# A mixed attention and expert kernel: W2 of all experts kept in SBUF, one pipeline round fewer in the GELU stage, and the SiLU stage's scores brought by transfers instead of matmuls

## What is computed

```python
t = t + landmark_attention(ln(t))       # 16 landmarks, 6 Newton steps for an inverse
t = t + ffn_gelu(ln(t))                 # 8 experts, top 2 of each token
t = t + dense_attention(ln(t))
t = t + ffn_silu(ln(t))                 # 2 shared and 16 routed experts, top 6

def ffn_gelu(xt):                       # T tokens, E=8, H=512
    gate = softmax(xt @ Wg)
    topv, topi = top_k(gate, 2)
    topv = topv / (sum(topv) + 1e-6)    # scores[token, expert]
    for e in range(8):
        h = gelu(xt @ W1[e] + b1[e])    # 128 -> 512
        out += (h @ W2[e] + b2[e]) * scores[:, e]

def ffn_silu(x):                        # 16 routed experts of 64 hidden units
    p = topk_normed(softmax(router(x)), 6)     # with a capacity for each expert
    out += (silu(x @ w_gate[e]) * (x @ w_up[e]) * score[:, e]) @ w_down[e]
    out += shared_experts(x) / 2
```

## Time and profile before

| | us |
|---|---|
| median of 3 runs (6106.2, 6124.97, 6126.56) | 6124.97 |
| the profiled execution's own time | 6120.88 |
| its span in the trace | 6119.1 |
| PE busy (share of the span) | 5094.9 (83%) |
| DVE busy | 3714.2 (61%) |
| ACT busy | 2975.9 (49%) |
| POOL busy | 900.7 (15%) |
| GELU stage up to its first round of tiles | 2617.5 to 2877.2 |
| GELU stage, rounds of tiles | 2877.2 to 4232.0 |
| SiLU stage | about 4262 to 6119.1 |

### The profile page before, as it was taken

The page is one execution under the profiler, slowest core; times in us unless marked ns, Lnnn a source line. Parts: engine busy times, 40 slices in busy tenths (PEclk is TensorE's granted clock), DMA queues, the critical chain, the costliest instruction groups (busy, mean ns, idle before and its releaser), DMA issues. The chain is left out here.

```text
span 6119.1 us, 86779 instructions
## 1 busy us (share of the span) xinstructions
PE 5094.9 (83%) x25888; PEld 2659.6 (43%) x25888; DVE 3714.2 (61%) x8142; ACT 2975.9 (49%) x5409; POOL 900.7 (15%) x1036
## 2 busy tenths in 40 slices
PE   3888888888888886946888888885699999999999
PEld 0222222222222221325878787874445455454453
DVE  4667666766666672645566656531566666666665
ACT  0555555555555553412555555553245454454552
POOL 1111111111111111202234334342000000000000
PEclk7999999999999998966999999998899999999999
DMA  3122212221121211232777778786100000000000
GB/s 125 51 81 76 63 63 83 63 63 63 63 74 63 77 56 32 29 83 78 216 249 250 231 234 258 232 250 215 45 4 5 5 3 5 5 5 5 3 5 9
DMA packets 370810, 538.97 MB, mean 88 GB/s; under 512 B 85897, under 2 KB 236737, under 8 KB 368497
## 3 DMA queue, kind: packets, MB, share of 16 engines
q1 hardware_dynamic: 350032, 501.28, 26.4%
q0 software_dynamic: 20576, 35.55, 2.0%
HBM read 357.79 MB, written 165.51 MB: 86 GB/s over the span
## 5 line engine op out<-in xcount | busy, mean ns | idle before, releaser
L523 ACT ACTIVATE a_probs<-ps_b 128x512 f32<-128x512 f32 x2048 | 1110.6, 595 | 967.4 <-PE ps_b L604 952.9
L409 DVE TENSOR_REDUCE a_negmax<-ps_a 128x1 f32<-128x1024 f32 x1024 | 1209.9, 1219 | 442.8 <-PE ps_a L552 409.4
L552 PE MATMUL ps_a<-a_k_stack,a_q_stack 96*128 96x512 bf16 x2048 | 663.3, 411 | 230.9 <-DVE a_negmax L409 126.3
L604 PE MATMUL ps_b<-a_q_stack,a_k_stack 99*128 99x512 bf16 x2048 | 704.6, 406 | 70.6 <-ACT a_probs L523 46.0
L1554 ACT ACTIVATE n_hidden<-n_ps_h,n_packs 128x128 f32<-128x128 f32 x1472 | 419.9, 370 | 379.4 <-PE n_ps_h L1728 378.4
L617 PE MATMUL ps_o<-a_probs,a_v_ones 128*32 128x512 f32 x4096 | 595.7, 656 | 0.2 <-ACT a_probs L523 0.2
L552 PEld LDWEIGHTS ps_a<-a_k_stack,a_q_stack 96*128 96x128 bf16 x2048 | 150.0, 101 | 819.0 <-DVE a_negmax L409 502.6
L1728 PE MATMUL n_ps_h<-n_xy,n_packs 128*128 128x128 f32 x2944 | 415.9, 286 | 68.5 <-DMA n_packs<-pack_scratch 67.7
L2021 ACT ACTIVATE e_act_up<-e_ps_g 128x512 f32<-128x512 f32 x288 | 172.0, 597 | 586.9 <-PE e_ps_g L2136 586.3
L604 PEld LDWEIGHTS ps_b<-a_q_stack,a_k_stack 99*128 99x128 bf16 x2048 | 200.0, 102 | 514.8 <-ACT a_probs L523 330.4
L1728 PEld LDWEIGHTS n_ps_h<-n_xy,n_packs 128*128 128x128 f32 x2944 | 374.2, 198 | 106.7 <-DMA n_packs<-pack_scratch 57.8
(11 more groups left out here) (323 smaller groups left out, 7277.4 us busy)
## 6 DMA issues: line engine op xcount, KB each, us to landing
n_packs<-pack_scratch SPq DMA_DIRECT2D x368, 514.0 KB
split_scratch<-a_pieces SPq DMA_DIRECT2D x192, 256.0 KB
a_q_stack<-split_scratch SPq DMA_DIRECT2D x128, 192.0 KB, 3.9
a_k_stack<-split_scratch SPq DMA_DIRECT2D x128, 192.0 KB, 4.4
rows_scratch<-n_zero SPq DMA_DIRECT2D x16, 1472.0 KB
outs_scratch<-n_xy SPq DMA_DIRECT2D x176, 128.0 KB
n_xg<-rows_scratch SPq DMA_DIRECT2D x80, 256.0 KB, 4.7
a_recips<-sums_scratch SPq DMA_DIRECT2D x64, 256.0 KB, 4.4
```

What stands on the lines that cost most here:

```text
L409: dve.tensor_reduce(negmax[:, b, t:t + 1], bank, axis=AX.X, op=ALU.max, negate=True).then_inc(ring_read, 1)
L523: act.activation(probs[:, m % PROBS, 512 * k:512 * k + 512], ps_b[:, k, :], ACT.Exp).then_inc(b_exp, 1)
L552: last = pe.matmul(bank[:, cols], q_stack[0:KS, h, 128 * t:128 * t + 128], k_stack[0:KS, h, cols], start=True, stop=True)
L604: pe.matmul(ps_b[:, k, :], k_stack[:, h, 128 * t:128 * t + 128], q_stack[:, h, 512 * k:512 * k + 512], start=True, stop=True).then_inc(b_u ...
```

## The change

**GELU weights.** W2 of all eight experts (down_weights) lies in SBUF for the whole stage, loaded once by eight transfers. b1 comes in one transfer and is turned by PE and copied by ACT. A tile's transfer brings only W1 (256 KB, up_weights, ring of four), straight from the input, and waits only for the up pass of the tile four earlier. pack_scratch, its building and the 32 loads of b1 are gone. Which expert a tile has, PE and ACT now read themselves. DVE adds up eight owners times powers of eight into one word (three words an image, owner_codes), PE and ACT load a word into a register before every eighth tile, and each tile shifts and masks it. With that they form, at run time, the address of W2 (a down pass's moving operand) and of the bias.

**One round fewer.** front(0); front(1) with choice(0); then rounds 0 to 13 with front(i+2) and choice(i+1), round 14 with choice(15), round 15 alone. combine(i−1) comes at the end of round i (slots 35 to 43). choice starts at slot 0 on DVE. The slot numbers of all pieces move; SP's list of what to do beside which tile follows. k1 and e3 share the buffers of xln and xt.

**SiLU scores.** The pieces, the selectors, the matmul b and score_now are gone. The scores are turned as they are, SP stores them to score_scratch in DRAM, and for each routed unit two transfers of 2 KB rows, each broadcast to 64 partitions, fill one of four buffers (256 KB in all). DVE multiplies by that buffer. SP's program for this is written out without a loop.

```diff
@@ GELU stage
-        packs = sb("packs", [128, RING, PACK])
+        up_weights, down_weights = sb("up_weights", [128, RING, F]), sb("down_weights", [128, E, FT, C])
+        b1_in = sb("b1_in", [E * FT, C])
...
         def pipeline(engine, front, choice, experts, begin=None):
             side_by_side([front(0)])
             side_by_side([front(1), choice(0)])
-            side_by_side([front(2), choice(1)])
             if begin:
                 begin()
-            for i in range(2):
-                experts(i, [front(i + 3), choice(i + 2)])
-            with engine.Fori(2, B - 3) as i:
-                experts(i, [front(i + 3), choice(i + 2)])
-            experts(B - 3, [choice(B - 1)])
-            experts(B - 2, [])
+            experts(0, [front(2), choice(1)])
+            with engine.Fori(1, B - 2) as i:
+                experts(i, [front(i + 2), choice(i + 1)])
+            experts(B - 2, [choice(B - 1)])
             experts(B - 1, [])
...
+        def owners_of(engine, i, word):
+            if isinstance(i, int):
+                return engine.value_load(owner_codes[0:1, i, word:word + 1], min_val=0, max_val=8 ** 8 - 1)
...
@@ SP
-            for dst, src in params:
-                sp.dma_start(dst, src).then_inc(params_in, 16)
...
+            load(0)
+            for dst, src in params:
+                sp.dma_start(dst, src).then_inc(params_in, 16)
...
             def load_pack(i, j):
                 if j >= RING:
-                    sp.wait_ge(y_ps, after(i, j - RING))
+                    sp.wait_ge(h_ps, after(i, j - RING))
...
-                sp.dma_start(packs[:, j % RING, :], pack_dram[bass.ds(e, 1), :, :].rearrange("e p f -> (e p) f")).then_inc(pack_in[j % RING], 16)
+                sp.dma_start(up_weights[:, j % RING, :], io["L2_ffn_W1"][bass.ds(e, 1), :, :].rearrange("e p f -> (e p) f")).then_inc(pack_in[j % RING], 16)
...
-                    if j == 20 and i + 1 < B:
-                        load_group(i + 1, 0)
...
+                if i + 1 < B:
+                    load_group(i + 1, 0)
@@ DVE
             def choice(i):
-                yield 11
+                yield 0
                 if started(i):
                     dve.wait_ge(scattered, i * 256)
                 token_norm(dve, xln2, tok, stats, mv, var, inv, tmp).then_inc(S["ln2_up"], 1)
...
+                dve.tensor_tensor(coded[:, :], owner[:, :], octal[:, :], ALU.mult)
+                dve.drain()
+                dve.tensor_reduce(owner[:, 0:WORDS], coded[:, :].rearrange("p (w t) -> p w t", t=8), axis=AX.X, op=ALU.add)
...
@@ PE
             def down(i, j):
...
+                own_down = down_weights[:, bass.ds(expert(j), 1), :, :].rearrange("p e t c -> p (e t) c")
                 for f in range(FT):
-                    last = pe.matmul(ps_xy[:, col:col + 128], hidden[:, j % 2, f, :], packs[:, j % RING, F + 128 * f:F + 128 * f + 128], start=(f == 0), stop=(f == FT - 1))
+                    last = pe.matmul(ps_xy[:, col:col + 128], hidden[:, j % 2, f, :], own_down[:, f, :], start=(f == 0), stop=(f == FT - 1))
...
                     if slot == 0 and started(i):
+                        if not isinstance(i, int):
+                            packed[2] = codes(i - 1, 2)
                         down(i - 1, LAST)
+                    if slot == 0:
+                        pe.wait_ge(S["owner_up"], i + 1)
+                    if slot % 16 == 0:
+                        packed[slot // 16] = codes(i, slot // 16)
@@ SiLU stage, SP
+            def load_scores(i, k, unit):
+                if unit >= RING:
+                    sp.wait_ge(mixed_up, i * STEPS + k * UNITS + unit - RING + 1)
...
+                for e in range(2):
+                    sp.dma_start(scores[64 * e:64 * e + 64, unit % RING, :],
+                                 score_dram[i, 2 * unit + e:2 * unit + e + 1, 512 * k:512 * k + 512].broadcast_to((64, 512))).then_inc(scores_in[unit % RING], 16)
@@ DVE
-                for p in range(PIECES):
-                    dve.drain()
-                    dve.tensor_copy(score_bf[:, :, :], gate["score"][:, :, :])
-                    dve.drain()
-                    dve.tensor_copy(score_pieces[:, :, E * p:E * p + E], score_bf[:, :, :])
-                    dve.tensor_tensor(gate["score"][:, :, :], gate["score"][:, :, :], score_bf[:, :, :], ALU.subtract)
...
-                        dve.tensor_tensor(mixed[:, n % 2, :], act_up[:, n % 2, :], ps_b[:, :], ALU.mult).then_inc(mixed_up, 1)
+                        dve.tensor_tensor(mixed[:, n % 2, :], act_up[:, n % 2, :], scores[:, unit % RING, :], ALU.mult).then_inc(mixed_up, 1)
@@ PE
-                            pe.matmul(ps_b[:, :], pairsel[:, 128 * unit:128 * unit + 128], score_now[:, cols], start=True, stop=True).then_inc(b_ps, 1)
```

More of the change, by code:

```diff
@@ L1460, in choice @@
                 dve.drain()
-                steps = routing(i)
-                for slot in range(34, 37):
-                    next(steps)
-                    yield slot
+                for n, _ in enumerate(routing(i)):
+                    if n % 2:
+                        yield 23 + n // 2
+                dve.drain().then_inc(S["owner_up"], 1)
                 for k in range(HALVES):
+                    yield 32 + 2 * k
                     dve.wait_ge(S["b2_ps"], i * HALVES + k + 1)
@@ L1503, in _ @@
             dve.wait_ge(params_in, 16 * len(params))
[L1504 to L1505 removed]
+            pipeline(dve, front, choice, experts, lambda: take_up(0))
             side_by_side([combine(B - 1)])
@@ L1866, in _ @@
-            with sp.Fori(0, B) as i:
-                for k in range(HALVES):
-                    sp.wait_ge(result_up, i * HALVES + k + 2)
-                    sp.dma_start(out[bass.ds(i, 1), :, 512 * k:512 * k + 512].rearrange("a c n -> (a c) n"), result[:, k, :]).then_inc(stored[k], 16)
+            for i in range(1, B):
+                sp.wait_ge(tok_in, i * 16)
+                load_tokens(i)
+            store_scores(0)
+            for i in range(B):
+                for k in range(HALVES):
+                    for unit in range(PAIRS):
+                        load_scores(i, k, unit)
+                        if k == 0 and unit == RING and i:
+                            store_result(i - 1, 1)
+                        if k == 1 and unit == RING:
+                            store_result(i, 0)
+                        if k == 1 and unit == RING + 1 and i + 1 < B:
+                            store_scores(i + 1)
@@ L2107, in choice @@
                 for t in range(NT):
-                    last = pe.transpose(pb[:, 128 * t:128 * t + 128], score_pieces[:, t, :], ident)
+                    last = pe.transpose(pb[0:E, 128 * t:128 * t + 128], gate["score"][:, t, :], ident)
                 last.then_inc(S["st_ps"], 1)
```

295 lines of the change are left out of this document (158 added, 137 removed).

## The result

The changed kernel takes 5954.74 us (median of 4, 5944.33 to 5962.41) against 6121.68 for the kernel before (median of 4). The ratio is 0.9739, with a 95% interval of 0.9714 to 0.9765: 167 us less, where 222 were forecast. The time lies inside the range that was given (5825 to 5985), but 55 us above the forecast of 5900 and outside the forecast's own spread (5865 to 5940). The profiled execution took 5955.96, its span is 5953.7.

What follows compares the result with a forecast made beforehand. PE was taken to bound the GELU rounds with side work and the SiLU rounds, transfers the bare GELU rounds. Start −15.6, warm-up −81.9, GELU rounds −19.8, SiLU −105 sum to −222.3, forecast 5900 us, range 5825 to 5985.

Steps and rivals of the forecast that it cites:

- The warm-up round: Before the GELU tiles: one 83.6 us round goes, front(2) and choice(1) moving beside round 0; +1.7 for hand-overs, sum −81.9 us.
- The loop round: GELU rounds with side work: PE's 88.4 us falls by 0.9 to 87.5, 14 rounds making 1225; bounds 84.5 and 94.
- (a): GELU loop round: a tile brings 256 KB instead of 514, so PE's wait for packs goes, −2.6 us.
- (b): GELU loop round: choice's norm first on DVE; PE waits for x2, +1.0 us, and the n_xln wait goes, −2.2.
- (c): GELU loop round: gate steps and running sums before counts and first Newton steps, +2.5 us; later Newton steps −1.4, counts −0.7.
- (d): GELU loop round: PE loads four code words into registers, +1.1 us, or 0 if the queue hides it.
- (e): GELU loop round: PE works out four down-pass addresses a tile at run time, 0.06 us a tile, +1.4 a round.
- rival C: SiLU rounds: DVE takes over as the attention's work fills freed time, gain there only 54 us, total 5950; chance 0.12.
- The SiLU stage: One bf16 matmul less in each of 256 units: −87 us in 14 rounds, −16.6 last two, −2 start; sum −105.
- Rival B: GELU tiles: PE's sequencer binds, run-time addresses costing 0.24 us a tile unhidden, +88 us, total 5988; chance 0.13.
- Rival D: GELU loop: next image's rows come late, each round 20 us longer, +280, total 6180, slower than before; chance 0.05.
- Rival F: More goes than forecast: SiLU stage −155 us and GELU loop rounds of 86, total 5830; chance 0.07.

Runs made afterwards that it cites:

- e1: Kernel before with only the GELU weights' part of the change, pipeline, slots and SiLU stage as before; 6098.35 us, ratio to before 0.998.
- e7: Changed kernel with x2 ahead of choice's norm, both Exps behind the move, k1's sum and reciprocal earlier, counts one slot later; 5902.51 us, ratio to before 0.9649.
- e3: Changed kernel without PE's word loads and run-time addresses, W2 at fixed addresses (choice of W2's expert left out); 5988.9 us, ratio to before 0.9803.
- e8: e7 with e3's edit, no word loads or run-time W2 addresses on PE; measured once, 5890.89 us.
- e4: Changed kernel with ACT's two Exps moved behind the move of rows (slots 11 to 13, 28 to 29); 5948.25 us, ratio to before 0.9743.
- e9: Changed kernel with choice's routing on DVE put back late, slots 37 to 45 instead of 23 to 31; measured once, 6245.43 us.
- e6: Changed kernel with two added 128x512 f32 matmuls a round ahead of PE's wait for x2, result overwritten; 5959.22 us, ratio to before 0.9753.

## Why the prediction was right, and where it was not

**The start** was right to 0.2 us (−15.4), and for the stated reason. **The warm-up round** was −78.1, not −81.9: what is left of the warm-up grew by 5.5 us instead of the 1.7 taken for the b1 table's hand-overs. In e1, which has the table and the old pipeline, it grew by 2.6 (234.4 to 237.0).

**The loop round** is the step that failed: 90.6 instead of 87.5, 43 of the 67 us that are missing; its own sign of being right was 86 to 89. By its terms, in the mean of ten rounds: (a) −2.6 for the packs and (b)'s −2.2 for n_xln came as said. (b)'s wait for x2 was mis-sized, 2.5 instead of 1.0; DVE had x2 ready 10.0 us into PE's round (3418.5 in the round from 3408.5) and not 13.3, because the transpose and the first of the three map operations had been done ahead of the round (from 3405.6 on) and only two stood behind the norm, but PE had come to the place after 7.8 us and not after 11.5: a slot without side work is shorter than the mean of 1.92. (c) was mis-sized the other way (its 2.5 was called between one and two of the long waits and is less than one): the counts' wait grew by 0.6 and the Newton waits fell by 1.8, where the sum put +2.5 − 1.4 − 0.7. (d) and (e), 2.5 together, measure 1.9 to 2.2: 1.4 to 1.5 by the last column (76.6 against 75.1 and 76.8 against 75.4), and 0.45 to 0.9 of PE's idle time that is put down to "issue" (4.5 us in ten rounds of the changed kernel, 5.0 and 3.9 of e7) and gone in e3 and e8. From the kernel before to e1 the same sum is only 1.0.

The largest miss is a term that was not there: the wait for the move of rows, which PE's next down pass needs, grew by 3.0 a round. ACT's two Exps, each with table loads around it, stand ahead of that move at slots 11 and 28 (22 and 26 before), and with e4's slots 2.7 of the 3.0 are gone. The slots are not all of it, since in e1, which has the old ones, this wait had already grown by 1.5. Nor is it a price of 3.0: in e4 the round fell by 0.2 only. The prediction went through DVE's and PE's pieces slot by slot and not through ACT's. And no term priced the clock: 3.9 us a round at half clock before, 5.9 after, 1.0 us a round.

**The order itself.** e1 shows that the sum's way of subtracting waits was unsafe: 2.6 us of pack waits removed with every slot left alone gave nothing. **Rounds 14 and 15** were 4 us longer than forecast each (63.0 for 59, 55.4 for 51), and the way from there to the SiLU stage 1 us shorter than before.

**Luck.** That the time fell inside the range owes something to luck: it lies beside rival C's 5950, and C's mechanism did not cause it. The terms of the loop round missed in both directions, up to 3 us each, where their sum was off by 3.1.

**The SiLU stage** was mis-sized by 13 us of 105, for a mechanism that was right: the last round fell by 8.1 (8.3 forecast), so b does cost 0.51 a unit where PE is the bound. The round before it was called bare too, but fell by 5.0: PE waits three times for e_mixed in it, 3.43 + 0.48 + 0.26 us before and 3.93 + 1.20 + 0.78 after. In the loop the gain is 5.5 a round where 6.2 was forecast and 8.3 were possible. The waits for e_mixed and e_act_up grew by 31.9 us in fourteen rounds, 2.3 each, close to the 2.1 of the four units that were taken as gaining nothing. That fits rival C in small: DVE takes back part of what PE gives where its work is dense.

**Rival B** (the sequencer binds) fell with e3 and e8: some 2 us a round, not 5.5. Its sign, down matmuls further apart than up matmuls, is absent where they run undisturbed:

```profile
3413.21 1.06 PE L1756 MATMUL n_ps_h<-n_xy,n_up_weights 128*128 128x128 f32 x8
3414.11 1.06 PE L1766 MATMUL n_ps_xy<-n_down_weights,n_hidden 128*128 x8
```

PE's queue in the trace has the steps themselves (duration in ns as min/median/max; the word load, then the down pass):

```profile
L1156 PEldq FUSED_REGOPS  x91: 46/151/156, 2861.7 to 4010.6; - x91
...
L1156 PEldq TENSOR_LOAD <-n_owner_codes x52: 297/310/990, 2861.3 to 4010.3; - x52
```

```profile
L1766 PEldq FUSED_REGOPS  x920: 46/46/51, 3049.8 to 3945.3; - x184
L1766 PEldq ALU_OP  x430: 36/36/36, 3049.7 to 3944.8; - x144
```

A register load is 310 ns here in the median, not the 600 that the Trainium skill ("DMA: Bandwidth & Descriptors", "Latency and other measured facts") calls the floor. The four address steps of 46 ns a tile pass mostly beside the matmuls. The prediction's other argument against B was worked out short. The Trainium skill ("TensorE: Matmul & The Clock Gate", "Back-to-back issue gap") gives its 62 ns for a MATMUL, with hardware decode off, and none for a weight load. The trace has two MATMUL and two weight load records for each 128x128 f32 matmul (x8 for four). With 62 ns for each of these and a step of 46 the estimate from the page's figure is 294 ns and not 181, more than the 0.22 us in which such matmuls follow each other here (the two rows above start 0.90 us apart for four), so it did not speak against B; the runs do. **Rival D** did not occur and e9 gives its price. **Rival F** did not occur in this kernel; e7's rounds of 86.4 come near it.

## What to carry to other kernels

When pieces of a hand-laid order move, go through every engine's pieces against the one hand-over that the busiest engine needs next, also on engines that are half idle; here the wait for a copy of 0.6 us by ACT grew by 3.0 us a round, more than the 2.6 that halving the weights' transfers had taken away. A wait that is removed is a gain only if the engine does not then wait at the next place (e1, e4), so price the sum of its waits, not one line. A wait of PE can cost twice, once as idle time and again in the clock behind it. Here that befell many of those of about two microseconds and more, not all of them, and of the versions that compute everything the one that waited least (e7) also had the least time at half clock, 41.0 us against 81.9.

## What was not expected of the hardware

Taking work away from PE made the kernel slower. e3, with four word loads and 92 address steps a round fewer, ran its loop at a mean clock of 0.93 instead of 0.97 and took 92.9 us a round instead of 90.0; on top of e7 the same edit gained 0.3 us a round. The reverse held as well: 1.72 us of added matmuls cost 0.1 us a round (e6). And unchanged code moved: the attention and convolution ahead of the GELU stage ended anywhere from 2607.2 to 2634.5 us, and in e1 the SiLU loop of the kernel before took 1584.0 us instead of 1565.8, with 146.8 instead of 122.9 us at half clock.
